# Layer 2 mixer of a four-layer network on one core: the causal convolution as four TensorE products with tap-scaled matrices, the gate product on GpSimd, and ScalarE's preparation part at the end of each step

## The reference, cut to what matters

```
xi, z = split(xn @ W_in)                      # 128 -> 256 + 256
xc    = silu(causal_depthwise_conv4(xi) + conv_b)
dt_lo, B, C = split(xc @ W_xp)                # 8 + 16 + 16
delta = softplus(dt_lo @ W_dt + dt_bias)
h     = h * exp(delta * A) + (delta * xc) * B # a scan over time, 16 states for each of 256 channels
y     = sum_over_states(h * C) + xc * D_skip
out   = (y * silu(z)) @ W_out
```

## Time and profile before

| what | value |
|---|---|
| median of 3 runs | 4549.53 us |
| lowest and highest run | 4514.15 and 4550.23 us |
| the profiled execution's own time | 4547.62 us |
| its span from first to last instruction | 4546.0 us |
| mean granted TensorE clock | 0.798 of full speed |

### The profile page before, as it was taken

The page is one execution under the profiler, slowest core; times in us unless marked ns, Lnnn a source line. Parts: engine busy times, 40 slices in busy tenths (PEclk is TensorE's granted clock), DMA queues, the critical chain, the costliest instruction groups (busy, mean ns, idle before and its releaser), DMA issues. The chain is left out here.

```text
span 4546.0 us, 51664 instructions
## 1 busy us (share of the span) xinstructions
PE 3301.8 (73%) x18282; PEld 1782.4 (39%) x18378; DVE 2601.4 (57%) x3680; ACT 1786.4 (39%) x3620; POOL 1274.6 (28%) x991
## 2 busy tenths in 40 slices
PE   6888888884437777777677676776767767677687
PEld 3444444442313333333334343343433434334343
DVE  3444444442746777777666555565656656566555
ACT  2333333331324444444334344343443434434344
POOL 0000000002323333333353242442424424244242
PEclk8888888886557777777879678797887978879779
DMA  2000000001212222222200000000000000000000
GB/s 85 7 7 7 7 7 5 7 2 58 94 45 64 69 69 69 69 69 67 71 1 6 8 5 3 5 5 8 5 3 5 5 8 5 3 5 5 8 2 6
DMA packets 82190, 111.61 MB, mean 25 GB/s; under 512 B 9920, under 2 KB 47296, under 8 KB 81472
## 3 DMA queue, kind: packets, MB, share of 16 engines
q1 hardware_dynamic: 76608, 97.85, 7.2%
q0 software_dynamic: 5376, 11.02, 0.9%
HBM read 82.09 MB, written 26.74 MB: 24 GB/s over the span
## 5 line engine op out<-in xcount | busy, mean ns | idle before, releaser
L369 ACT ACTIVATE l_PT<-PB 128x512 f32<-128x512 f32 x512 | 277.9, 595 | 547.4 <-PE PB L280 547.4
L280 PE MATMUL PB<-l_QM,l_KP 32*128 32x256 f32 x2048 | 376.5, 498 | 131.7 <-DVE l_QM L418 76.0
L1413 POOL TENSOR_TENSOR l_ST<-l_ST,l_CT 128x1024 f32<-128x1024 f32 x128 | 304.6, 2379 | 525.7 <-DVE l_ST L1358 525.7
L407 DVE TENSOR_REDUCE keep_MXP<-PB 128x4 f32<-128x1024 f32 x256 | 301.3, 1219 | 110.2 <-PE PB L253 110.2
L280 PEld LDWEIGHTS PB<-l_QM,l_KP 32*128 32x128 f32 x2048 | 242.4, 244 | 256.6 <-ACT l_PT L369 99.9
L1358 DVE TENSOR_TENSOR_SCAN l_ST<-l_DA,l_DB 128x1024 f32<-128x1024 f32 x128 | 338.8, 2647 | 4.4
L1563 POOL TENSOR_TENSOR l_PT<-l_PT,l_PEN 128x512 f32<-128x512 f32 x168 | 212.5, 1285 | 189.7 <-ACT l_PT L369 189.7
L703 POOL MEMSET l_KV<- 128x4 f32 x8 | 0.8, 105 | 921.3 <-POOLq L109 921.3
L1352 DVE TENSOR_TENSOR l_DB<-PB,l_BT 128x1024 f32<-128x1024 f32 x128 | 155.6, 1216 | 179.7 <-PE PB L1102 179.3
L1827 POOL TENSOR_TENSOR l3f_SQ<-l3f_RW 128x512 f32<-128x512 f32 x128 | 146.9, 1148 | 312.5 <-ACT l3f_RW L1693 312.5
L1102 PE MATMUL PB<-l_DL,consts 32*128 32x512 f32 x512 | 192.6, 779 | 53.9 <-DVE l_DB L1352 39.3
(11 more groups left out here) (414 smaller groups left out, 7207.7 us busy)
## 6 DMA issues: line engine op xcount, KB each, us to landing
l_WB<-in_w2f_dram SPq DMA_DIRECT2D x80, 320.0 KB, 3.0
l_WB<-in_w2f_dram SPq DMA_DIRECT2D x80, 258.0 KB, 2.7
l_XR<-xs_mid SPq DMA_DIRECT2D x80, 64.0 KB, 1.8
ys_mid<-l_YO SPq DMA_DIRECT2D x80, 64.0 KB, 2.9
s_mid<-keep_S SPq DMA_DIRECT2D x17, 256.0 KB, 2.0
w3fs<-in_w3f_dram SPq DMA_DIRECT2D x1, 3125.0 KB, 17.4
keep_XI<-in_x_dram SPq DMA_DIRECT2D x9, 256.0 KB, 3.2
x_mid<-keep_X SPq DMA_DIRECT2D x9, 256.0 KB, 3.3
```

The source lines that it names most:

```text
L280: last = nc.tensor.matmul(PB[:, 4 + u % STBANKS, kt * SEQ:(kt + 1) * SEQ], b.KP[rows, a, i, k0:k0 + 128], b.QM[rows, n % 2, :], start=True ...
L369: nc.scalar.activation(b.PT[:, u % PSLOTS].rearrange("p k q -> p (k q)"), PB[:, 4 + u % STBANKS, :], ACT.Exp).then_inc(s.exp_done, 1)
L407: nc.vector.tensor_reduce(dst[:, 2 * pair:2 * pair + 2, :, 16 + n % 2], PB[:, 2 * pair:2 * pair + 2, :].rearrange("p r (t k) -> p r t k", ...
L1413: nc.gpsimd.tensor_tensor(b.ST[:, g % RING], b.ST[:, g % RING], b.CT[:, k % 2, :].unsqueeze(1).broadcast_to([128, 2, T]), ALU.mult).then_i ...
```

## The change

TensorE now multiplies the normalised input, kept in a buffer `XM` with three zero columns ahead of each sequence, by four matrices per half, each being W_in's xi part with its columns scaled by one tap of the convolution. The four products, each with the input shifted by one column more, add up in PSUM. The scaled matrices are made once by one VectorE product (`taps_ready`) from taps that the host lays out over 128 partitions, so that the weight block `w2s` grows by 1016 columns. ScalarE adds the bias while it empties the bank, into `XC`. The z products come first (steps 3 and 4), the convolution products in steps 5 and 6, and all later TensorE and ScalarE pieces one step earlier than before (W_xp in 8, delta in 9 and 10, B in 11, C in 12). The convolution on VectorE goes, with the copies into `XI`. The two silu instructions of the halves of `XC` become one. The squaring of the layernorm's reciprocal root moves from VectorE to ScalarE. The gate product moves to GpSimd, in two halves: the first in step 10 of the chunk, the second in step 2 of the next one, each ahead of the step's product with C. `take_sums` moves ahead of the step's `drive`, and `project` from step 3 to step 2. ScalarE's preparation piece of step n now stands last in step n, where the one of step n - 1 stood in the middle.

The core of the diff (the renamed semaphores and the host's layout of the taps are left out):

```diff
+W2 = [("g", 1), ("b", 1), ("win", 2 * 2 * 128), ("conv", TAPS * DI), ("cb", 2), ("xp", 2 * 96), ("dt", DI),
...
-        b = buffers(nc, ctx, "l2", XN=[3, T], XM=[T], XI=[2, NB, TAPS - 1 + SEQ], XC=[2, 2, T], ZS=[2, 2, T], DL=[2, 2, T], DU=[2, 2, T],
...
@@ -1065,33 +1067,39 @@
                         if h == 0:
...
                         else:
-                            pe.wait_ge(s.xi_copied, 2 * k + 1)
-                        nc.tensor.matmul(PB[:, LANE, :], w.win[:, h * 128:(h + 1) * 128], b.XM[:], start=True, stop=True).then_inc(s.xz_ready, 1)
+                            pe.wait_ge(s.z_copied, 2 * k + 1)
+                        nc.tensor.matmul(seq(PB[:, LANE, :]), w.win[:, (2 + h) * 128:(3 + h) * 128], XS, start=True, stop=True).then_inc(s.xz_ready, 1)
...
-                            pe.wait_ge(s.xi_copied, 2 * k + 2)
+                            pe.wait_ge(s.z_copied, 2 * k + 2)
+                            if k == 0:
+                                pe.wait_ge(s.taps_ready, 1)
+                                pe.wait_ge(s.pads_set, 1)
                         else:
-                            pe.wait_ge(s.z_copied, 2 * k + 1)
-                        nc.tensor.matmul(PB[:, LANE, :], w.win[:, (2 + h) * 128:(3 + h) * 128], b.XM[:], start=True, stop=True).then_inc(s.xz_ready, 1)
-                    elif step == 9:
-                        pe.wait_ge(s.z_copied, 2 * k + 2)
-                        pe.wait_ge(s.silu_x, 2 * k + 2)
+                            pe.wait_ge(s.x_copied, 2 * k + 1)
+                        for tap in range(TAPS):
+                            last = nc.tensor.matmul(seq(PB[:, LANE, :]), w.conv[:, tap * DI + h * 128:tap * DI + (h + 1) * 128], b.XM[:, :, tap:tap + SEQ],
+                                                    start=tap == 0, stop=tap == TAPS - 1)
+                        last.then_inc(s.conv_ready, 1)
+                    elif step == 8:
+                        pe.wait_ge(s.x_copied, 2 * k + 2)
+                        pe.wait_ge(s.silu_x, k + 1)
                         for h in range(2):
                             last = nc.tensor.matmul(PB[0:96, LANE, :], w.xp[:, h * 96:(h + 1) * 96], b.XC[:, p, h, :], start=h == 0, stop=h == 1)
                         last.then_inc(s.xd_ready, 1)
...
 
                 def project(k):
-                    pe.wait_ge(s.y_gated, k + 1)
+                    pe.wait_ge(s.y_gated, 2 * k + 2)
                     pe.wait_ge(s.hid_done, 4 * SLOTS * (k + 1))
                     for h in range(2):
                         last = nc.tensor.matmul(PB[:, WORK, :], w.out[:, h * 128:(h + 1) * 128], b.YG[:, h, :], start=h == 0, stop=h == 1)
...
-                        if n == 3 and k:
+                        if n == 2 and k:
                             project(k - 1)
...
@@ -1209,33 +1217,32 @@
                     elif step == 1:
                         act.wait_ge(s.ln_var, k + 1)
                         link(nc.scalar.activation(c.lnr[:], PB[:, SMALL, :], ACT.Ln, bias=c.eps))
-                        nc.scalar.activation(c.lnr[:], c.lnr[:], ACT.Exp, scale=-0.5).then_inc(s.ln_rstd, 1)
+                        link(nc.scalar.activation(c.lnr[:], c.lnr[:], ACT.Exp, scale=-0.5))
+                        nc.scalar.activation(c.lnt[:], c.lnr[:], ACT.Square).then_inc(s.ln_rstd, 1)
...
+                        if k >= 2 and h == 0:
+                            act.wait_ge(s.y_gated, 2 * (k - 1))
+                        act.wait_ge(s.xz_ready, 2 * k + h + 1)
+                        nc.scalar.activation(b.ZS[:, p, h, :], PB[:, LANE, :], ACT.Copy).then_inc(s.z_copied, 1)
...
+                            act.wait_ge(s.y_taken, 2 * (k - 1))
+                            act.wait_ge(s.drive_ready, k - 1)
+                        act.wait_ge(s.conv_ready, 2 * k + h + 1)
+                        nc.scalar.activation(b.XC[:, p, h, :], PB[:, LANE, :], ACT.Identity, bias=w.cb[:, h:h + 1]).then_inc(s.x_copied, 1)
                     elif step == 7:
                         act.wait_ge(s.z_copied, 2 * k + 2)
+                        act.wait_ge(s.x_copied, 2 * k + 2)
                         link(nc.scalar.activation(b.ZS[:, p], b.ZS[:, p], ACT.Silu))
-                        for h in range(2):
-                            act.wait_ge(s.conv_done, 2 * k + h + 1)
-                            nc.scalar.activation(b.XC[:, p, h, :], b.XC[:, p, h, :], ACT.Silu).then_inc(s.silu_x, 1)
+                        nc.scalar.activation(b.XC[:, p], b.XC[:, p], ACT.Silu).then_inc(s.silu_x, 1)
                         act.preload_act_table_set(EXP_LN)
...
+                    elif step == 11:
+                        act.wait_ge(s.b_spread, k + 1)
+                        if k >= 2:
+                            act.wait_ge(s.part_ready, PAIRS * (k - 1))
+                        nc.scalar.activation(b.BT[:, p, :], PB[:, LANE, :], ACT.Copy).then_inc(s.b_copied, 1)
                     elif step == 12:
                         act.preload_act_table_set(LN)
                         act.wait_ge(s.dt_error, k + 1)
                         nc.scalar.activation(b.UU[:], b.UU[:], ACT.Ln).then_inc(s.dt_log, 1)
                         act.preload_act_table_set(EXP_LN)
-                        act.wait_ge(s.b_spread, k + 1)
-                        if k >= 2:
-                            act.wait_ge(s.part_ready, PAIRS * (k - 1))
-                        nc.scalar.activation(b.BT[:, p, :], PB[:, LANE, :], ACT.Copy).then_inc(s.b_copied, 1)
-                    elif step == 13:
                         act.wait_ge(s.c_spread, k + 1)
                         nc.scalar.activation(b.CT[:, p, :], PB[:, LANE, :], ACT.Copy).then_inc(s.c_copied, 1)
...
@@ -1296,12 +1303,12 @@
                             tile_out(j - 2)
                         if PAIRS * k + n + 1 < PAIRS * CHUNKS:
                             decay(PAIRS * k + n + 1)
-                        if n and k + 1 < CHUNKS:
-                            head(k + 1, n - 1)
                         if FIRST + 1 <= n < FIRST + 1 + SLOTS:
                             tile_hidden(j - 1)
                         if FIRST <= n < FIRST + SLOTS:
                             tile_rows(j)
+                        if k + 1 < CHUNKS:
+                            head(k + 1, n)
...
                         if k:
...
-                        link(nc.vector.tensor_tensor(u, v, v, ALU.mult))
+                            dve.wait_ge(s.conv_ready, 2 * k)
+                        v, u = c.lnr[:], c.lnt[:]
                         link(nc.vector.scalar_tensor_tensor(out=u, in0=PB[:, SMALL, :], scalar=c.eps, in1=u, op0=ALU.add, op1=ALU.mult))
                         link(nc.vector.scalar_tensor_tensor(out=u, in0=u, scalar=-3.0, in1=v, op0=ALU.add, op1=ALU.mult))
-                        link(nc.vector.scalar_tensor_tensor(out=b.XM[:], in0=ctr, scalar=-0.5, in1=u, op0=ALU.mult, op1=ALU.mult))
-                        nc.vector.tensor_scalar(b.XM[:], b.XM[:], w.g, w.b, ALU.mult, ALU.add).then_inc(s.xm_ready, 1)
...
-                        h = step - 4
...
-                        link(nc.vector.tensor_scalar(xc, b.XI[:, h, :, 0:SEQ], w.conv[:, h * TAPS:h * TAPS + 1], w.cb[:, h:h + 1], ALU.mult, ALU.add))
-                        for tap in range(1, TAPS):
-                            last = nc.vector.scalar_tensor_tensor(out=xc, in0=b.XI[:, h, :, tap:tap + SEQ],
-                                                                  scalar=w.conv[:, h * TAPS + tap:h * TAPS + tap + 1], in1=xc, op0=ALU.mult, op1=ALU.add)
-                            if tap < TAPS - 1:
-                                link(last)
-                        last.then_inc(s.conv_done, 1)
-                    elif step == 12:
+                        link(nc.vector.scalar_tensor_tensor(out=XS, in0=seq(PB[:, LANE, :]), scalar=-0.5, in1=seq(u), op0=ALU.mult, op1=ALU.mult))
+                        nc.vector.tensor_scalar(XS, XS, w.g, w.b, ALU.mult, ALU.add).then_inc(s.xm_ready, 1)
...
                 def take_sums(k, h):
                     dve.wait_ge(s.y_added, PAIRS // 2 * k + PAIRS // 4 * (h + 1))
+                    if k and h == 0:
+                        dve.wait_ge(s.mamba_ready, k)
                     nc.vector.scalar_tensor_tensor(out=b.YG[:, h, :], in0=b.XC[:, k % 2, h, :], scalar=w.dskip[:, h:h + 1], in1=PB[:, SUMS, :],
                                                    op0=ALU.mult, op1=ALU.add).then_inc(s.y_taken, 1)
-
-                def gated(k):
-                    dve.wait_ge(s.y_taken, 2 * k + 2)
-                    nc.vector.tensor_tensor(b.YG[:], b.YG[:], b.ZS[:, k % 2], ALU.mult).then_inc(s.y_gated, 1)
...
+                taps = w.conv.rearrange("p (a d) -> p a d", d=DI)
+                nc.vector.tensor_tensor(taps, taps, w.win[:, 0:DI].unsqueeze(1).broadcast_to([128, TAPS, DI]), ALU.mult).then_inc(s.taps_ready, 1)
                 for step in range(PAIRS):
                     head(0, step)
                 for k in range(CHUNKS):
```

(24 more changed lines are left out.)

39 lines of the change are left out of this document (12 added, 27 removed).

## The result

The changed kernel takes 4405.74 us (median of 4 runs, 4399.17 to 4421.23) against 4549.88 for the one before (4 runs, 4514.15 to 4552.05). The ratio is 0.971, 95% interval 0.967 to 0.975: 2.9% faster. The forecast was 4477 us with a range of 4425 to 4560. The direction was right and the gain, 144 us, is twice the 72 that were forecast and outside the range. The profiled execution took 4399.17 us, its span is 4397.5.

A forecast was written before the change was run, and what follows sets the result against it. Waits between engines bound the kernel, with TensorE's clock a second cost. Seven chunks gain 81.9 us and chunk 7 1.7, less 10 for first preparation and 1.3 for loading: net 72.3 off 4547.6; median 1.9 higher, so 4477, range 4425 to 4560.

The forecast's parts named there:

- The layout by steps: One chunk at full clock, new order: steps 5 to 12 take 50.9 us, steps 13 to 4 45.6, together 96.5.
- The first rival: Gap of step 8 too short to cost TensorE's clock: 4446 us; chance 0.20.
- the steps 5 and 6: TensorE's pieces plus one convolution block at the end of each step: 7.6 us and 8.1 us.
- the clock term: TensorE's 1.9 us gap in step 8 costs one slow stretch per chunk, 4.4 us: 96.5 becomes 100.9.
- The convolution block: Four accumulated TensorE products per half, in steps 5 and 6, each 1.06 us: 4.25 us a block.
- step 13: Two VectorE delta instructions and GpSimd's product exclude each other after the scan: 8.5 us between drive products.
- The first preparation: Uncovered preparation before the first chunk, at 1.2 GHz: 10 us longer, between 0 and 11.3.
- The gate term: Gate product moved to GpSimd in halves: step 2 takes 9.5 us; chunk 7, with take_sums and add_input moved, gains 1.7.
- The split between the blocks: Waits behind ScalarE's blocks: 5.2 us at step 9 (silu), near 4 at step 13 (Ln), 9 of 11.7 per chunk.
- the load of the larger weights: Loading before the first work: 1016 more columns, 0.52 MB, cost 1.3 us more.
- The slow rivals: Convolution at 1.2 GHz: 4571 us, chance 0.14; TensorE at 1.2 GHz through steps 5 to 12: 4699 us, chance 0.06.

The follow-up runs named there:

- all but the convolution: Kernel before plus ScalarE's pieces at the end of their step and the gate product on GpSimd, convolution still on VectorE: chunk period 98.4 us.
- only the later pieces last: Kernel before with only ScalarE's preparation pieces of steps 10 to 13 (softplus, Ln) at the end of their step, silu unmoved: period 104.9 us, a gain of 7.7.

## Why the prediction was right or wrong

**The layout by steps was right, and its total close.** 96.5 us were laid out, 91.7 were measured, and six of the eight pairs of steps lie within 0.7 us. The first rival, "TensorE never loses the clock", is nearly the case that came, and its own figure, 4446 us, is 40 above the 4406 measured. So the mechanism was read rightly in the main (ScalarE's blocks behind what TensorE waits for, the convolution as a block on TensorE), and three terms of the sum were not: the clock, the steps 5 and 6, and the preparation.

**The step that failed first is the clock term: "I take one such loss per chunk: 100.9".** The gap of 1.85 us is there in every chunk, and in five of seven the clock stayed at 2.4 GHz through it. In the two others step 8 is 9.0 and 9.1 instead of 7.6: the slow stretch is near 3 us long and not 9, so it costs 1.5 us and not 4.4. The term was 7 x 4.4 = 30.8 us, and 2.9 were paid. The rows named for the loss had waits of 5.22 us and more; no row put a price on a gap of 2 us, and I had said so against the rival instead of against the forecast. The loss was not an idle fear: in the run with all but the convolution a gap of 1.95 us at the same place was followed by a slow stretch in each of the seven chunks. What spares the changed kernel, the blocks ahead of the gap or the product right behind it, is open.

**The convolution block, "4 x 1.06 = 4.25", was mis-sized.** It is 3.53, and a second one behind it adds 3.4. The 1.06 was the spacing from one product to a different piece behind it. The earlier trace rows held the better reading: two products in a row took 3.70 where one took 2.07 at 1.2 GHz, so a further one costs 1.63, or 0.82 at full clock. Steps 5 and 6 are 12.8, not 15.7, and the two blocks are 1.4 of these 2.9 us. Another 1.3 is a lead that the layout left out. TensorE's spread for step 5 starts 2.65 us ahead of that step's drive product (1748.15 against 1750.80), the one for step 7 only 1.36 (1762.21 against 1763.57): TensorE enters step 5 ahead and spends the lead, so the time between the drive products is shorter than its own work. All 2.9 x 7 make 20 us.

**The other steps are 2.3 us shorter together**: of the 9.2 by which the period missed, 4.0 are the clock term and 2.9 the steps 5 and 6. In the table, steps 11 and 12 are shorter by 1.1, 13 and 14 by 0.7, 7 and 8 by 0.6, with small differences of both signs elsewhere. In step 13 the mechanism was the forecast one. VectorE's second delta instruction waits for GpSimd's product (3.25 us, where it had 1.22 alone):

```profile
1798.52 2.29 DVE L1350 TENSOR_TENSOR_SCAN l_ST<-l_DA,l_DB 128x1024 f32<-128x1024 f32 x1
1800.73 1.20 DVE L1333 TENSOR_TENSOR l_EE<-l_UU,l_EE 128x1024 f32<-128x1024 f32 x1
1800.89 3.24 POOL L1411 TENSOR_TENSOR l_ST<-l_ST,l_CT 128x1024 f32<-128x1024 f32 x1 [2.49 <-DVE l_ST L1350]
1801.96 3.25 DVE L1334 SCALAR_TENSOR_TENSOR l_DL<-l_DL,l_EE 128x1024 f32<-128x1024 f32 x1
1805.14 1.21 DVE L1344 TENSOR_TENSOR l_DB<-PB,l_BT 128x1024 f32<-128x1024 f32 x1
```

The first one slipped in ahead of GpSimd's product, whose 3.24 us (2.35 alone) hold a wait for it; I had put both behind it. The step takes 7.9, not 8.5.

**The first preparation was over-priced.** From the first layernorm product (1304.76, before 1309.98) to the first drive product it is 52.8 us against 49.1: 3.6 more, not 10. On TensorE's timeline:

```profile
1320.03 6.18 PE L1082 MATMUL PB<-l_XM,w2s 128*128 128x512 f32 x8 [0.69 <-ACT l_ZS L1227]
1326.99 3.70 PE L1082 MATMUL PB<-l_XM,w2s 128*128 128x512 f32 x8 [0.78 <-ACT l_XC L1234]
```

The two blocks take 9.9 us, where I had put twice 7.4 for the 11.3 and 3.3 less with the second at full clock. From the first input product to the W_xp product it is 5.8 us more (1314.51 to 1335.08, before 1319.80 to 1334.55), and behind it 2.1 less, where I had put nothing.

**The gate term had the wrong sign.** Chunk 7 was to gain 1.7 and lost 2.8; the run without the gate's move is at 72.0. The rule cited in the prediction (the Trainium skill, Perfetto Trace Analysis, "Optimizing Scalar/DVE Operations": moving work between VectorE and GpSimd might not help) was right against my sum, and the runs agree: 91.7 with and without the move, 112.6 with and without it, 98.4 with it and 98.7 without. In the fourth pair the move costs: the changed kernel with the order undone has 108.1 with it and 105.5 without.

**The split between the blocks was off.** I put 5.2 us on the wait of step 9 and near 4 on that of step 13. By the run with only the later pieces last, softplus and Ln bring 7.7, and silu and the rest another 6.2 on top of them.

**The sum.** In the profiled executions 72.3 were forecast and 148.5 came (4546.0 - 4397.5). The period accounts for 64.4 of the difference (7 x 9.2), the preparation for 6.4, chunk 7 for -4.5. The remaining 9.9 lie outside the mixer's steps: the preparation began 5.2 us earlier, although the load of the larger weights was to cost 1.3, and the part after the last drive product was 3.4 shorter. No run explains these, and the same code varies by more elsewhere.

The slow rivals did not come: over steps 3 to 8 the granted clock is 1.00 in four chunks, 0.95 in the two where it falls in step 8, and 0.92 in chunk 0.

## What to carry to other kernels

In a loop of steps that engines share by hand-written order, put the long pieces of a side chain last on their engine, behind what another engine waits for in the next step: two moved lines brought two thirds of this gain (13.9 of 20.9). A wait removed in front of TensorE is worth its length and also the slow stretch behind it, so price it at both, and expect a small edit far away to move the slow stretch instead of ending it. Before moving an elementwise product from VectorE to GpSimd, look whether the two already exclude each other in the trace.

## What the runs showed of the hardware that I had not expected

- A gap of 1.85 us in TensorE's work left the granted clock at 1.00 in five of seven chunks. With less work ahead of it and more short gaps behind it (all but the convolution), one of 1.95 us was followed by a slow stretch in seven of seven, with 0.66 in the worst steps.
- Accumulating float32 products of 128x512 follow each other at 0.86 us at 2.4 GHz, against 1.06 from a single product to a different piece.
- Work that nothing reads, put into a wait (22 bfloat16 products of 128x512), made a chunk of the kernel before shorter by 3.8 us, by the clock alone.
- A GpSimd product that starts while a scan runs on VectorE does not stop it: the scan ended at 1736.50 and the product, of 1.26 us at its shortest, at 1737.55. Either order of arrival makes the later one wait.
